# Quantizing x's tiles every 16 pieces from unit 5 on, with the multiply on ScalarE and the magic addition on GpSimd

## The reference

```python
xn = layernorm(x)
s  = attention(xn, wq, wk, wv, wo)      # 32 query heads of 16, one key/value head, causal
g  = silu(linear8bit(linear8bit(xn, W1, b1), W2, b2))
x  = x + s * g

def linear8bit(x, W, b):
    outlier = max(abs(x), over rows) > 3.0         # per column
    x_in, x_out = where(outlier, 0, x), where(outlier, x, 0)
    return quant_rows(x_in) @ quant_rows(W).T + x_out @ W.T + b

def quant_rows(a):
    scale = max(max(abs(a), axis=-1) / 127, 1e-8)
    return clip(round(a / scale), -127, 127) * scale
```

## Time and profile before

| | |
|---|---|
| median of 3 runs | 774.07 us (772.74 to 776.4) |
| the profiled execution | 773.78 us, its span 772.1 us |
| TensorE (PE) busy | 736.0 us, 95% of the span |
| VectorE (DVE) busy | 635.6 us, 82% |
| ScalarE (ACT) busy | 398.3 us, 52% |
| GpSimd (POOL) busy | 295.6 us, 38% |

### The profile page before, as it was taken

How to read it: one execution, slowest core, us unless ns; L and a number is a source line. 1 busy time by engine, 2 the same in 40 slices (tenths; PEclk the granted TensorE clock), 3 DMA queues, 4 the chain that set the end, 5 groups by cost and what they waited for, 6 DMA issues and landing times. The chain is left out here.

```text
span 772.1 us, 11989 instructions
## 1 busy us (share of the span) xinstructions
PE 736.0 (95%) x4133; PEld 560.6 (73%) x4133; DVE 635.6 (82%) x1080; ACT 398.3 (52%) x681; POOL 295.6 (38%) x369
## 2 busy tenths in 40 slices
PE   4998999999999999999999999999998999999995
PEld 3887765656666777765678878788876888888884
DVE  7878999998999999995548588597869998599957
ACT  4653566766676777777634445454463333132312
POOL 7557445555555555554622222122100000127404
PEclk9999999999999999999999999999999999999998
DMA  7542123222323333344455766555315588337972
GB/s 259 161 168 60 40 54 88 72 73 85 85 85 91 97 90 90 86 122 144 145 191 155 205 218 183 184 118 151 83 44 195 199 257 271 124 93 252 323 287 109
DMA packets 93772, 110.71 MB, mean 143 GB/s; under 512 B 43136, under 2 KB 50320, under 8 KB 92176
## 3 DMA queue, kind: packets, MB, share of 16 engines
q1 hardware_dynamic: 93712, 109.95, 46.8%
HBM read 56.43 MB, written 40.37 MB: 125 GB/s over the span
## 5 line engine op out<-in xcount | busy, mean ns | idle before, releaser
L1024 DVE TENSOR_REDUCE rowmax<-ps 128x2 f32<-128x512 f32 (+3 forms) x384 | 211.5, 589 | 20.4 <-PE ps L1137 18.0
L946 ACT ACTIVATE probs<-ps 128x512 f32<-128x512 f32 (+1 forms) x352 | 174.4, 561 | 66.5 <-PE ps L1152 65.3
L1137 PE MATMUL ps<-km,stack 128*128 128x256 f32 (+3 forms) x512 | 142.5, 325 | 2.8 <-PEq L236 2.1
L1152 PE MATMUL ps<-stack,ks 128*128 128x512 f32 (+1 forms) x352 | 131.8, 383 | 4.4 <-ACT probs L946 3.4
L1137 PEld LDWEIGHTS ps<-km,stack 128*128 128x128 f32 (+1 forms) x512 | 92.2, 189 | 36.6 <-DVE rowmax L1024 19.4
L899 POOL TENSOR_SCALAR_AFFINE_SELECT probs<-probs 128x512 f32<-128x512 f32 x128 | 80.6, 638 | 55.8 <-ACT probs L946 55.0
L2019 PE MATMUL ps<-big_h 128*128 128x512 f32 x256 | 100.0, 390 | 2.0 <-DVE big_l L1835 1.6
L2020 PE MATMUL ps<-big_l,big_h 128*128 128x512 f32 x256 | 99.6, 389 | 0.0
L2021 PE MATMUL ps<-big_h,big_l 128*128 128x512 f32 x256 | 99.6, 389 | 0.0
L1167 PE MATMUL ps<-probs,vones 128*32 128x512 f32 (+3 forms) x1024 | 82.2, 439 | 0.2 <-POOL probs L899 0.2
L1152 PEld LDWEIGHTS ps<-stack,ks 128*128 128x128 f32 x352 | 66.4, 189 | 14.4 <-ACT probs L946 7.2
(11 more groups left out here) (234 smaller groups left out, 1377.6 us busy)
## 6 DMA issues: line engine op xcount, KB each, us to landing
stack<-big_h SPq DMA_DIRECT2D x128, 64.0 KB, 2.0
h_scratch<-hs SPq DMA_DIRECT2D x7, 1024.0 KB, 4.7
hload<-h_scratch SPq DMA_DIRECT2D x14, 512.0 KB, 5.3
xn_scratch<-xa SPq DMA_DIRECT2D x4, 1024.0 KB, 4.6
stack<-big_l SPq DMA_DIRECT2D x64, 64.0 KB, 2.0
xi<-xn_scratch SPq DMA_DIRECT2D x16, 256.0 KB, 2.7
xe_scratch<-xm SPq DMA_DIRECT2D x16, 256.0 KB, 2.3
w2n<-in_L_ffn_W_dram SPq DMA_DIRECT2D x4, 1024.0 KB, 6.7
```

Of the source, the lines that this page charges most:

```text
L946: nc.scalar.activation(probs[p][:, o:o + nh * w], ps[:, STB[n % NST], 0:nh * w], ACT.Exp).then_inc(s_exp, 1)
L1024: nc.vector.tensor_reduce(dst, src, AX_X, ALU.max).then_inc(s_red, 1)
L1137: last = nc.tensor.matmul(dst, stack[u % 3][rows, hp, P * qt:P * (qt + 1)], km[rows, u // KT, p0:p0 + npar, keys], start=True, stop=True)
L1152: ins = nc.tensor.matmul(ps[:, STB[n % NST], 0:nh * w].rearrange("p (h q) -> p h q", h=nh), ks[:, u // KT, p, P * kt:P * (kt + 1)], stack[ ...
```

## The change

The tiles of x are no longer tied to units. Tile i meets step 157 + 16 i plus an offset: load 1, mask 8, maximum 11, scale 12, reciprocal 13, multiply 15, magic addition 16, rounding 17, scaling back 19, store 20. So the first tile is loaded at step 158 and stored at 177, the last loaded at 398 and stored at 417 (before: the first at 34 and 65, the last at 394 and 425). VectorE's multiply-add of line 783 is gone; ScalarE multiplies xi by the reciprocal into xm, and GpSimd adds the magic row in a new instruction in front of its rounding. Since 16 isn't a divisor of 24, the places of a tile repeat every three tiles:

| tiles | load | mask | maximum, scale, reciprocal | multiply | magic, rounding | back | store |
|---|---|---|---|---|---|---|---|
| 0, 3, 6, 9, 12, 15 | 14 | 21 | 0, 1, 2 | 4 | 5, 6 | 8 | 9 |
| 1, 4, 7, 10, 13 | 6 | 13 | 16, 17, 18 | 20 | 21, 22 | 0 | 1 |
| 2, 5, 8, 11, 14 | 22 | 5 | 8, 9, 10 | 12 | 13, 14 | 16 | 17 |

The loads of xi (x's next tile, and W1's first) now wait for ScalarE's multiply, counted on a semaphore that an earlier stage has left at 2.

```diff
+        s_xf = s_wkvz
+        KV_ZEROED = 2
...
-        XLOAD_AT, XMASK_AT, XSCALE_AT, XROUND_AT, XBACK_AT, XSTORE_AT = -1, 15, 21, 25, 26, 30
+        XFIRST, XSTEP = 157, 16
+        XLOAD_AT, XMASK_AT, XSCALE_AT, XTIMES_AT, XMAGIC_AT, XROUND_AT, XBACK_AT, XSTORE_AT = 1, 8, 11, 15, 16, 17, 19, 20
...
+        def x_tile_at(g, at):
+            i, r = divmod(g - XFIRST - at, XSTEP)
+            return i if r == 0 and 0 <= i < NT else -1
...
-                if part == 3:
-                    dve.wait_ge(s_xst, 3 * i + 3)
-                    nc.vector.scalar_tensor_tensor(out=xm[:, :], in0=xi[:, :], scalar=xs[:, 0:1],
-                                                   in1=magic_row[:, :], op0=ALU.mult,
-                                                   op1=ALU.add).then_inc(s_xt, 1)
...
-                    u = unit_at(g, XLOAD_AT)
+                    u = x_tile_at(g, XLOAD_AT)
                     if u >= 0:
                         if u:
-                            sp.wait_ge(s_xt, u)
+                            sp.wait_ge(s_xf, KV_ZEROED + u)
                         sp.dma_start(xi[:, :], xn_d[P * u:P * (u + 1), :]).then_inc(s_xl, 16)
-                    u = unit_at(g, XSTORE_AT)
+                    u = x_tile_at(g, XSTORE_AT)
...
-                    if unit_at(g, XSTORE_AT + 1) == U - 1:
+                    if x_tile_at(g, XSTORE_AT + 1) == NT - 1:
...
                     if unit_at(g, W1_LOAD_AT) == U - 1:
-                        sp.wait_ge(s_xt, NT)
+                        sp.wait_ge(s_xf, KV_ZEROED + NT)
...
-                    u = unit_at(g, XMASK_AT)
+                    u = x_tile_at(g, XMASK_AT)
...
-                    u = unit_at(g, XROUND_AT)
+                    u = x_tile_at(g, XMAGIC_AT)
+                    if u >= 0:
+                        pool.wait_ge(s_xf, KV_ZEROED + u + 1)
+                        nc.gpsimd.tensor_tensor(xm[:, :], xm[:, :], magic_row[:, :], ALU.add).then_inc(s_xt, 1)
+                    u = x_tile_at(g, XROUND_AT)
...
-                    u = unit_at(g, XBACK_AT)
+                    u = x_tile_at(g, XTIMES_AT)
+                    if u >= 0:
+                        act.wait_ge(s_xst, 3 * u + 3)
+                        nc.scalar.mul(xm[:, :], xi[:, :], xs[:, 0:1]).then_inc(s_xf, 1)
+                    u = x_tile_at(g, XBACK_AT)
...
-                    for part in range(4):
-                        if unit_at(g, XSCALE_AT + part) >= 0:
-                            quantize_x(dve, unit_at(g, XSCALE_AT + part), part)
+                    for part in range(3):
+                        if x_tile_at(g, XSCALE_AT + part) >= 0:
+                            quantize_x(dve, x_tile_at(g, XSCALE_AT + part), part)
```

## The result

The changed kernel takes **802.49 us** (median of 4 runs, 800.88 to 804.83) against 774.85 us for the kernel before (4 runs, 772.74 to 776.4). The ratio is 1.0357, with a 95% interval of 1.0336 to 1.0378. It is 27.6 us slower; the forecast was 14.9 slower, and its range ended at 797. The direction was right, the size was not.

What follows compares the result with a forecast made beforehand. VectorE was taken to bound the early attention units, TensorE the late ones. Losses of 20.3 us (12.5 + 2.0 + 1.6 + 2.5 + 1.7) less 5.4 gained gave 14.9, from 773.8 to about 788.5 us, range 775 to 797.

Steps and rivals of the forecast that it cites:

- early units: Units 0 to 4, where VectorE loses work: gain 1.3 us per unit; 5.4 us in all, bounds 2.8 and 7.0.
- the tail: End of the attention stage: tile 15's multiply and additions among the last exponentials and selects, 1.7 us (0 to 3.3).
- Tiles 1, 4, 7, 10, 13: Additions at places 21 and 22 delay ScalarE's scaling back at place 0, then TensorE: 2.5 us each, 12.5 in all.
- inside the same delay: Select behind the magic addition also keeps the second product with the values waiting, but at no added cost.
- Tiles 0, 3, 6, 9, 12: Maximum at place 0 stands ahead of the reductions of places 1 to 3: 0.4 us, five times, 2.0.
- masking at place 21: GpSimd's masking of tiles 3, 6, 9, 12 delays the second select: 0.4 us, four times, 1.6.
- The lock: VectorE instruction with two SBUF inputs and GpSimd SBUF reads exclude each other: 0.4 us a tile, 2 us, outside the sum.
- Tiles 2, 5, 8, 11, 14: ScalarE's scaling back at place 16 comes just ahead of an exponential: 0.5 us, five times, 2.5.
- floor of 15.5: TensorE's time for an early unit: late unit's 18.3 us less 2.8 us of projection, against 17.2 us then.
- (a): Faster: GpSimd and ScalarE find room, TensorE sees no wait in the late half, early gain stays: 768.4 us; 13%.
- (b): One wait only: just the tiles at place 20 cost, the rest hides: 2.6 to 7.1 us, about 778; 20%.
- (c): Early units give nothing, since TensorE and ScalarE hold them at 17.2 us: 794 us; 12%.

Runs made afterwards that it cites:

- x11: Changed kernel with all wide steps on x's tiles, except tile 0's masking, on one column; 774.37 us, ratio 0.9996 to the kernel before.
- x10: x9 plus ScalarE's scaling back of tiles 2, 5, 8, 11, 14 on one column; 780.02 us, ratio 1.0066 to the kernel before.
- x2: Changed kernel with both GpSimd additions of tiles 1, 4, 7, 10, 13 on one column; 787.82 us, ratio 1.0160 to the kernel before.
- x8: Changed kernel without ScalarE's scaling back of tiles 1, 4, 7, 10, 13, additions kept; 793.59 us, ratio 1.0243 to the kernel before.
- x1: Changed kernel with GpSimd's masking of tiles 3, 6, 9, 12, 15 on one column; 797.11 us, ratio 1.0273 to the kernel before.
- x9: x3 plus VectorE's maximum of x on one column in every tile; 781.62 us, ratio 1.0086 to the kernel before.
- x5: Changed kernel with masking of tiles 3, 6, 9, 12 replaced by a 1024-column GpSimd write and a one-column masking; 804.41 us, one run, no ratio.
- x3: Changed kernel with the narrow masking of x1 and the narrow additions of x2 together; 784.20 us, ratio 1.0105 to the kernel before.
- x6: Changed kernel's split of the multiply-add, but one tile per unit near the old places; 773.55 us, ratio 0.9976 to the kernel before.
- x7: Changed kernel with every step of every tile of x two steps earlier; 792.51 us, ratio 1.0241 to the kernel before.
- x4: Changed kernel's moved tiles, but VectorE keeps its multiply-add at the new multiply's place; 791.21 us, ratio 1.0196 to the kernel before.

## Why the prediction was wrong, and where it was right

**Where the missing 13 us lie.** By the traces the change loses 13.2 us more than forecast. In the terms of the sum: the early units gain 2.3 us less; unit 7 loses 1.9 more; each of the four pairs from unit 8 on loses 5.0 to 5.1 us where the sum has 3.8 (2.5 + 0.4 + 0.4 + 0.5), and units 12 and 13 another 1.3, which matches one stretch at half clock; the tail loses 4.4 more; start and FFN give 1.8 back. Of the 1.3 us too little per pair, 0.35 are in the steps that the sum prices. The other 0.95 are in steps for which it has no term: the multiplies, the additions and maskings of the other tiles (0.7 by x11 against x10), and what is left with all of them narrow (0.25).

**Tiles 1, 4, 7, 10, 13: the size right in the units, the path only in part.** Forecast 2.5 us per tile; x2 measures 2.0 in units 8 to 11. Queue order, length of GpSimd's work and ScalarE's wait came as written. The failed half of the step is its sentence that the late select lies "inside the same delay": x8 shows that with ScalarE's wait gone 0.8 of the 2.0 us stay, and its rows show the select, and VectorE's cast and subtraction beside the additions, late as well. These are parallel paths of nearly the same length, which makes each look like the cause.

**Tiles 0, 3, 6, 9, 12: the step that failed.** The forecast priced the maximum at place 0 by VectorE's own time, 0.4 us past a spare of 0.37, and never asked whether its input would be there. The masking stands at place 21, behind the low part and a select, and ends after VectorE has come to place 0. In units 7 and 13 it waits 0.88 and 0.85 us; in the others, VectorE is already held by the lock, which ends at the same moment. The price list treated "masking at place 21" only as a delay of the next select, 0.4 us a tile; x1 measures 1.1 us in units 10 and 11, and unit 7, where tile 0's masking stays whole in x11, is still 1.6 us over before there. The price of the maximum itself, 0.4, held: narrow maxima (x9) give back about 0.4 in each of units 9 and 11. The five units with a maximum at place 0 lose 7.9 us in place of 2.0; 1.1 of these, in unit 13, are a delay that falls in the unit before it where the lock holds VectorE, and in unit 12 the lock was just missed.

**The lock, left out of the sum.** The prediction gave 2 us to it and set it aside. In the trace it costs VectorE 1.31 instead of 0.17 us at three places, and 0.7 more in the cast at others. x5 shows that taking it away at the masking gains almost nothing while the maximum waits for the masking, so it was no simple extra term; at the additions it stands in one of the parallel paths, and what it is worth there alone no run shows.

**Tiles 2, 5, 8, 11, 14: right.** Forecast 0.5 us per tile; x10 took 0.45 off each of units 8 and 10.

**The tail: mis-sized, and the cause in part open.** Forecast 4.7 (tile 15 1.7, tile 13 2.5, tile 14 0.5), measured 9.1. The tails of the kernel before, of the changed one and of x8 (window, its length, then busy us and instructions of TensorE, its weight loads, VectorE, ScalarE and GpSimd, clock, DMA):

```profile
349.59:393.41 43.82, 40.33 (x271) 27.03 (x270) 22.04 (x42) 28.00 (x56) 20.13 (x26) 1.00 0.42 136
...
369.94:422.87 52.93, 46.29 (x270) 29.59 (x270) 21.32 (x40) 29.66 (x59) 24.71 (x30) 0.87 0.38 119
...
363.53:411.24 47.71, 41.17 (x271) 26.58 (x270) 21.30 (x40) 28.99 (x58) 24.66 (x30) 1.00 0.41 132
```

TensorE's idle time grew by 3.1 us and its busy time by 6.0. In x8, which lacks only tile 13's scaling back here and whose clock held, idle time grew as much (3.0) and busy time by 0.8; the lengths of the matmuls add up to 104.9, 118.3 and 105.1 us in the three. So by x8 the waits are no more than the forecast's 4.7, and the rest, matmuls that take longer, goes with the 13.6 us at half clock in this tail. In x3, whose clock held too, and where the additions of tile 13 and the masking of tile 15 are narrow, 2.6 us are left, against 2.2 forecast for tiles 14 and 15. The end of the changed kernel, ScalarE, GpSimd, TensorE; it answers to the earlier trace rows:

```profile
403.10 0.71 ACT L962 ACTIVATE xm<-xi,xs 128x512 f32<-128x512 f32 x1
...
403.89 1.28 POOL L874 TENSOR_TENSOR xm<-xm,magic_row 128x512 f32<-128x512 f32 x1 [1.48 <-ACT xm L962]
405.12 0.64 POOL L905 TENSOR_SCALAR_AFFINE_SELECT probs<-probs 128x512 f32<-128x512 f32 x1
405.73 1.27 POOL L878 TENSOR_TENSOR xm<-xm,magic_row 128x512 f32<-128x512 f32 x1
...
404.97 4.50 PE L1177 MATMUL ps<-probs,vones 128*32 128x512 f32 x32
```

The additions stand among the selects as written; ahead of the multiply the maximum had waited 1.54 us for its masking (0.91 before), the question missed once more. What an execution without the half clock would win back stays open: the one whose clock held was only 1 to 4 us shorter in all than the other three (last section), and x5, with 6.8 us at half clock in place of 13.6, has a tail of 52.0.

**Early units: inside the bounds, at the lower end.** Forecast 1.3 us a unit (bounds 0.7 and 1.7), measured 0.8; in all 3.1 for 5.4. Two early units of the changed kernel (window, its length, then busy us and instructions by engine, clock, DMA):

```profile
113.83:146.63 32.80, 32.67 (x246) 20.30 (x245) 31.79 (x65) 23.04 (x49) 14.72 (x24) 1.00 0.22 51
```

TensorE is busy 32.67 of 32.80 us, 16.3 a unit. My floor of 15.5, the late unit less the projection, was not the one to take. The earlier trace rows already held the better one: 17.06 of 18 us busy is 16.3 in a unit of 17.2. The rule "take the engine's recorded busy time per unit as the floor" would have given 0.9.

**Rivals.** (a) came true in another kernel: x6 has its mechanism, with the places that (a) lacks, and gains 1.9 of its 5.4 us. (b) is out, since more than one wait costs. (c) named 794, and by size came closest, but for the wrong reason: the early units did gain.

**The range.** It was narrower than the prediction's own bounds. Prices of 2.0 to 3.4 at place 20 alone give 786 to 793, not 782 to 794, and all bounds of the terms of the sum added up, without the 1 us a tile for the queues, give 777 to 803. The measured 802.5 lies at the end where nearly every term is at its upper bound.

## What to carry to other kernels

Where engines wait in order, the place of an instruction can cost more than the engine that does it: here the same split was 0.24% faster near the old places, one tile to a unit, and with the move 3.6% slower. For each moved step walk two questions, not one: who stands behind it in its queue, and is its input ready when its engine comes there; the second was missed here. And where several paths to the same matmul are nearly equally late, removing one measures only its lead over the next, so shorten them together before giving each a price.

## What the runs showed of the hardware

- A short VectorE instruction beside a 1.28 us GpSimd addition or masking is held until that ends: 16 columns 1.31 us in place of 0.17, a cast of 32 columns 1.01 in place of some 0.3, a subtraction of 32 columns 1.23 in place of 0.19. Beside a GpSimd instruction that only writes it is not (0.17), and in unit 12 of the changed kernel, where it began 0.02 us ahead of the masking, it was not either (0.17; 0.01 ahead, at 264.80, it was held). For small two-input steps the length is set by the neighbour's, six to eight times their own.
- TensorE's granted clock fell to 0.50, the lower of its two levels (1.2 of 2.4 GHz), inside the attention stage of the changed kernel, where that of the kernel before stayed at 1.00. One such stretch, as window, length, busy times by engine and clock:

```profile
402.60:409.40 6.80, 6.60 (x38) 2.07 (x36) 0.82 (x3) 3.68 (x7) 4.28 (x5) 0.50 0.29 82
```

There are three, 3.4 us at 290.0 and 6.8 us at 375.3 and 402.6, the last two in the tail. Shortly before each TensorE had waited: 1.34 us until 289.91, 1.08 until 374.59, 0.83 until 401.88. A wait of 1.34 us until 248.19 was followed by none. Such stretches are not tied to the late units: x2, x3, x8, x10 and x11 have none before the last microseconds, x1, x5 and x7 have some among the late units, but x1, x4, x5 and x9 also have one at 66 to 68 us, and x6, x7 and x9 one in the FFN (498.2, 597.5 and 589.0), which the change doesn't touch. What brings them on stays open.

- What they cost can be read in units: unit 0 takes 18.1 to 18.3 us with a stretch of 3.4 us (x1, x4, x5, x9) and 16.75 without, 1.4 to 1.6 more; units 12 and 13 of the changed kernel take 1.3 more than units 10 and 11. Of the four executions of the changed kernel, the one with a mean clock of 0.996 had a span of 799.1 us, the others (0.986, 0.986, 0.989) 800.1, 803.1 and 801.4. So the clock's part in the 28 us is 1 to 4 by the spans, as far as one execution can tell, and 6 by the units and the tail of the profiled one (1.3 in units 12 and 13, 5.1 of busy time in the tail over that of x8).
